# A graph layer and routed experts on one core: six counted pieces, weighed six rows a step

## The reference

```python
mems2 = layernorm(x).at[y].set(r)
keep_w = (dst != y)                                    # edges into y are dropped
nbr = top_k(-sum((mems2 - r)**2), 7)                   # seven edges nearest -> y are added
deg = segment_sum(w, col) + 2.0
dinv = rsqrt(deg)
out = segment_sum(dinv[row] * w * dinv[col] * (mems2 @ W)[row], col) + 2 * dinv**2 * (mems2 @ W)
x = x + out
idx, prb = argmax and max of softmax(layernorm(x) @ gate_w + gate_b)
pos = rank of the token within its expert              # kept if below 1954 (capacity 1.25)
x = x + (relu(h @ w1[idx] + b1[idx]) @ w2[idx] + b2[idx]) * prb * kept
```

## Time and profile before

| | us |
|---|---|
| median of 3 runs | 2663.68 (2661.24 to 2668.46) |
| profiled execution | 2664.55 |
| its span, first to last instruction | 2662.9 |
| first gather of the node phase starts | 244.0 |
| last gather of the node phase starts | 1858.9 |
| POOL busy in the span | 1582.6 (59%) |
| PE busy in the span | 1940.1 (73%) |

### The profile page before, as it was taken

One profiled execution on the slowest core, in us unless ns is written; L12 is line 12 of the kernel. 1 busy time (PEld: TensorE's weight loads), 2 busy tenths in 40 slices (PEclk: granted clock), 3 DMA queues, 4 the chain that ended last, 5 costly groups with the idle time before them and its releaser, 6 DMA issues. The chain is left out here.

```text
span 2662.9 us, 37670 instructions
## 1 busy us (share of the span) xinstructions
PE 1940.1 (73%) x11184; PEld 1685.1 (63%) x11185; DVE 1355.6 (51%) x3909; ACT 616.2 (23%) x1239; POOL 1582.6 (59%) x1644
## 2 busy tenths in 40 slices
PE   2003667776677667767767789898599899899985
PEld 1003556765566556656656678887588688788775
DVE  7969886245622651452251257776444344345443
ACT  1467000210021002102102133333223332332222
POOL 6622677777777777777777777777123422422233
PEclk8556888998899889979989999999699899899988
DMA  9135233753366346536636677876412212211211
GB/s 276 46 89 166 85 102 114 212 179 103 102 194 208 102 123 202 178 101 192 211 108 208 196 225 205 217 206 168 146 33 71 80 37 69 73 39 67 66 42 26
DMA packets 240395, 350.66 MB, mean 132 GB/s; under 512 B 47464, under 2 KB 173576, under 8 KB 240068
## 3 DMA queue, kind: packets, MB, share of 16 engines
q0 software_dynamic: 75712, 198.29, 26.0%
q1 hardware_dynamic: 163172, 148.02, 19.0%
q10 hardware_dynamic: 1312, 2.10, 0.3%
HBM read 296.73 MB, written 56.40 MB: 133 GB/s over the span
## 5 line engine op out<-in xcount | busy, mean ns | idle before, releaser
L681 POOL DMA_INDIRECT arena<-z_table,arena x1248 | 1220.1, 978 | 482.6 <-issue 374.1
L1773 PE MATMUL bank<-arena 128*128 128x128 f32 x4992 | 734.6, 309 | 336.3 <-DMA arena<-z_table,arena 171.0
L1773 PEld LDWEIGHTS bank<-arena 128*128 128x128 f32 x4992 | 682.7, 219 | 432.7 <-issue 350.8
L1239 DVE TENSOR_TENSOR nodes<-nodes,bank 128x256 f32 x312 | 131.2, 421 | 781.9 <-PE bank L1773 768.8
L741 POOL DMA_INDIRECT out<-arena x128 | 130.1, 1017 | 437.5 <-DVE arena L1654 420.8
L2021 PE MATMUL bank<-arena 128*128 128x256 f32 (+1 forms) x1472 | 332.4, 386 | 29.3 <-issue 18.2
L2021 PEld LDWEIGHTS bank<-arena 128*128 128x128 f32 x1472 | 284.9, 197 | 70.4 <-issue 31.8
L2033 PE MATMUL bank<-arena,nodes 128*128 128x256 f32 (+1 forms) x1472 | 326.0, 380 | 0.0
L818 ACT ACTIVATE arena<-arena 128x512 f32<-128x512 uint16 (+1 forms) x125 | 135.4, 1086 | 810.7 <-DVE arena L1258 463.9
L2033 PEld LDWEIGHTS bank<-arena,nodes 128*128 128x128 f32 (+1 forms) x1472 | 273.2, 188 | 39.5 <-issue 1.0
L921 ACT ACTIVATE nodes<-bank,arena 128x256 f32<-128x256 f32 (+1 forms) x368 | 152.4, 465 | 467.1 <-PE bank L2021 467.1
(11 more groups left out here) (316 smaller groups left out, 1801.2 us busy)
## 6 DMA issues: line engine op xcount, KB each, us to landing
arena<-z_table SPq DMA_DIRECT2D x120, 512.0 KB
arena<-z_table,arena POOLq DMA_INDIRECT x1248
arena<-in_L_ffn_w SPq DMA_DIRECT2D x14, 1024.0 KB, 7.6
z_table<-nodes SPq DMA_DIRECT2D x14, 896.0 KB, 6.7
x_rows<-nodes SPq DMA_DIRECT2D x98, 128.0 KB
arena<-in_x SPq DMA_DIRECT2D x48, 256.0 KB, 3.7
out<-nodes SPq DMA_DIRECT2D x96, 128.0 KB
nodes<-in_x SPq DMA_DIRECT2D x12, 896.0 KB, 11.5
```

What stands on the lines that cost most here:

```text
L681: nc.gpsimd.indirect_dma_start(gath[:, slot, t, :], None, z_table, bass.IndirectOffsetOnAxis(ap=src_idx[:, tile_at:tile_at + 1], axis=0)). ...
L1239: nc.vector.tensor_tensor(where, where, agg_bank[step % AB][:, 0:D].rearrange("p (k c) -> p k c", k=KD), ALU.add).then_inc(S["agg_added"], 1)
L1773: last = nc.tensor.matmul(agg_bank[i][:, k * P:(k + 1) * P], gath[:, i, t, k * P:(k + 1) * P], sel[:, i, t, :], start=(t == 0), stop=(t == ...
```

## The change

`PIECES` becomes 144, 64, 48, 40, 32 and 24 tiles: 352 counted tiles in place of 320, and six pieces in place of five. `HB` becomes 6: six rows per chunk, 17 chunks (the last has two rows), 16 chunk steps per piece. Piece 0 is weighed, copied out and turned as the others are; node `y` takes the place of the 128th column, and the piece's strips are clipped one node lower. `count_f`, `near_row` and `piece_rows` leave the arena and lie over a new tensor `columns`, together with sixteen node vectors of the preparation and the routing that had tensors of their own. ACT waits for `res_ok` ahead of the experts.

```diff
-    PIECES = [144, 64, 48, 40, 24]
+    PIECES = [144, 64, 48, 40, 32, 24]
-    HB = 4
+    HB = 6
...
+        columns = sb("columns", [P, 16 * NW])
+        count_f = columns[:, 0:2 * HB * P].rearrange("p (j h n) -> p j h n", j=2, h=HB)
+        near_row = columns[0:1, 0:8 * P]
+        piece_rows = columns[:, 0:KD * P].rearrange("p (k c) -> p k c", k=KD)
+        (first_f, n_less, last_hist, deg, neg_mean, rstd, shift, var2, gap2, kept, pos_lo, pos_hi, expert,
+         pos_f, part_f, row_f_i) = [columns[:, i * NW:(i + 1) * NW] for i in range(16)]
...
@@ chunk_counts (ACT)
+                nodes_in = P - 1 if p == 0 else P
                 if p == 0:
                     act.wait_ge(S["chosen_ok"], 1)
-                    nc.scalar.activation(count_f[:, j, 0:m, P], chosen[:, c * HB:c * HB + m], ACT.Copy)
-                nc.scalar.activation(count_f[:, j, 0:m, 0:P], counts[:, :, c * HB:c * HB + m].rearrange("p n h -> p h n"),
+                    nc.scalar.activation(count_f[:, j, 0:m, P - 1], chosen[:, c * HB:c * HB + m], ACT.Copy)
+                nc.scalar.activation(count_f[:, j, 0:m, 0:nodes_in],
+                                     counts[:, 0:nodes_in, c * HB:c * HB + m].rearrange("p n h -> p h n"),
                                      ACT.Copy).then_inc(S["count_ok"], 1)
@@ pieces of a step (ACT)
-                    if p:
-                        take_piece(p)
+                    take_piece(p)
@@ ahead of the experts (ACT)
+            act.wait_ge(S["res_ok"], 2)
             act.sem_inc(S["hid_ok"], FT)
@@ unit limits (DVE)
-                then(nc.vector.tensor_scalar(unit_rel[0:1, mine], unit_rel[0:1, mine], float(P - PANEL), 0.0, ALU.min, ALU.max))
+                then(nc.vector.tensor_scalar(unit_rel[0:1, mine], unit_rel[0:1, mine], float(P - PANEL - (p == 0)), 0.0, ALU.min, ALU.max))
@@ add_piece (DVE)
-                if p == 0:
-                    dve.wait_ge(S["piece_ps"], 1)
-                    total = piece_bank[:, 0:KD * (P + 1)].rearrange("p (k c) -> p k c", k=KD)
-                else:
-                    dve.wait_ge(S["piece_turned"], p)
-                    total = piece_bank[:, D:2 * D].rearrange("p (k c) -> p k c", k=KD)
+                dve.wait_ge(S["piece_turned"], p + 1)
+                total = piece_bank[:, D:2 * D].rearrange("p (k c) -> p k c", k=KD)
...
@@ weigh_chunk (PE)
                 for i in range(m):
-                    if p:
-                        last = nc.tensor.matmul(piece_bank[:, 0:D], count_f[:, j, i, 0:P], z_ring[:, j, i, :], start=False, stop=False)
-                        continue
-                    for k in range(KD):
-                        last = nc.tensor.matmul(piece_bank[:, k * (P + 1):k * (P + 1) + width], z_ring[:, j, i, k * P:(k + 1) * P],
-                                                count_f[:, j, i, 0:width], start=False, stop=False)
+                    last = nc.tensor.matmul(piece_bank[:, 0:D], count_f[:, j, i, :], z_ring[:, j, i, :], start=False, stop=False)
...
@@ end of a piece (PE)
-                if p:
-                    turn_piece(p)
+                turn_piece(p)
```

More of the change, by code:

```diff
@@ L235, in build @@
         r_rows = sb("r_rows", [P, D])
+        columns = sb("columns", [P, 16 * NW])
[4 more added lines that the diff above has]
+         pos_f, part_f, row_f_i) = [columns[:, i * NW:(i + 1) * NW] for i in range(16)]
+        pos_i, part_i, row_i = pos_f.bitcast(I32), part_f.bitcast(I32), row_f_i.bitcast(I32)
+        assert 2 * HB * P <= 16 * NW
         y_i = sb("y_i", [P, 1], I32)
@@ L299, in build @@
         z_ring = carve([2, HB, D])
[L300 to L305, removed]
         at[0] = counts_at
@@ L409, in build @@
         EDGE_TURNS = [(i, b, min(4, EB - b)) for i in range(2) for b in range(0, EB, 4)]
-        neg_mean = sb("neg_mean", [P, NW])
-        rstd = sb("rstd", [P, NW])
-        shift = sb("shift", [P, NW])
         dist = sb("dist", [P, NW])
-        deg = sb("deg", [P, NW])
-        last_hist = sb("last_hist", [P, NW])
-        first_f = sb("first_f", [P, NW])
         first_i = sb("first_i", [P, NW], I32)
-        n_less = sb("n_less", [P, NW])
         row_start = sb("row_start", [P, NW + 1])
@@ L442, in build @@
         mean2 = neg_mean
-        var2 = sb("var2", [P, NW])
-        gap2 = sb("gap2", [P, NW])
         rstd2 = rstd
@@ L448, in build @@
         norm = n_less
-        expert = sb("expert", [P, NW])
         node_half = expert
         place = last_hist
-        kept = sb("kept", [P, NW])
-        row_i = sb("row_i", [P, NW], I32)
         row_f = sb("row_f", [P, NW])
[L455 to L458, removed]
         iota_r = sb("iota_r", [P, P])
@@ L1267, in add_piece @@
                 dve.wait_ge(S["agg_added"], adds_through(step))
-                if p == 0:
-                    dve.wait_ge(S["piece_ps"], 1)
-                    total = piece_bank[:, 0:KD * (P + 1)].rearrange("p (k c) -> p k c", k=KD)
-                else:
-                    dve.wait_ge(S["piece_turned"], p)
-                    total = piece_bank[:, D:2 * D].rearrange("p (k c) -> p k c", k=KD)
-                where = agg[:, :, bass.ds(base, P)]
-                nc.vector.tensor_tensor(where, where, total[:, :, 0:P], ALU.add).then_inc(S["agg_added"], 1)
+                dve.wait_ge(S["piece_turned"], p + 1)
+                total = piece_bank[:, D:2 * D].rearrange("p (k c) -> p k c", k=KD)
+                nodes_in = P - 1 if p == 0 else P
+                where = agg[:, :, bass.ds(base, nodes_in)]
+                nc.vector.tensor_tensor(where, where, total[:, :, 0:nodes_in], ALU.add).then_inc(S["agg_added"], 1)
                 if p == 0:
@@ L1278, in add_piece @@
                     own = agg[:, :, bass.ds(ycol, 1)]
-                    then(nc.vector.tensor_tensor(own, own, total[:, :, P:P + 1], ALU.add))
+                    then(nc.vector.tensor_tensor(own, own, total[:, :, P - 1:P], ALU.add))
             def x1_pair(b, j):
@@ L1790, in weigh_chunk @@
                 j = n % 2
-                width = P + 1 if p == 0 else P
                 pe.wait_ge(S["count_ok"], q * BODY + (n + 1))
@@ L1794, in weigh_chunk @@
                 for i in range(m):
-                    if p:
-                        last = nc.tensor.matmul(piece_bank[:, 0:D], count_f[:, j, i, 0:P], z_ring[:, j, i, :], start=False, stop=False)
-                        continue
-                    for k in range(KD):
-                        last = nc.tensor.matmul(piece_bank[:, k * (P + 1):k * (P + 1) + width], z_ring[:, j, i, k * P:(k + 1) * P],
-                                                count_f[:, j, i, 0:width], start=False, stop=False)
+                    last = nc.tensor.matmul(piece_bank[:, 0:D], count_f[:, j, i, :], z_ring[:, j, i, :], start=False, stop=False)
                 last.then_inc(S["chunk_ps"], 1)
             def turn_piece(p):
-                pe.wait_ge(S["piece_out"], p)
+                pe.wait_ge(S["piece_out"], p + 1)
                 for k in range(KD):
@@ L1810, in _ @@
             for p in range(NP):
-                span = KD * (P + 1) if p == 0 else D
-                whole = piece_bank[:, 0:span]
+                whole = piece_bank[:, 0:D]
                 s0, c0, n0 = strip_step[p], chunk_step[p], UNIT0[p]
@@ L1836, in _ @@
                     pe.wait_ge(S["chosen_ok"], 1)
-                nc.tensor.matmul(whole, zeros[:, 0:P], zeros[:, 0:span], start=True, stop=False)
+                nc.tensor.matmul(whole, zeros[:, 0:P], zeros[:, 0:D], start=True, stop=False)
                 with pe.Fori(0, (PCH - 1) // BODY - 1) as q:
@@ L1846, in _ @@
                 weigh_chunk(p, p * PCH + PCH - 1, 0, NW - (PCH - 1) * HB)
-                nc.tensor.matmul(whole, zeros[:, 0:P], zeros[:, 0:span], start=False, stop=True).then_inc(S["piece_ps"], 1)
-                if p:
-                    turn_piece(p)
+                nc.tensor.matmul(whole, zeros[:, 0:P], zeros[:, 0:D], start=False, stop=True).then_inc(S["piece_ps"], 1)
+                turn_piece(p)
             R_STEPS, R_PAIRS = 2 * BODY, 2 * PAIRS_IN[0]
```

## The result

| | us | ratio to before, 95% |
|---|---|---|
| before | 2663.68 (2660.41 to 2668.86) | |
| after | 2648.06 (2635.64 to 2649.03) | 0.993 [0.9911, 0.9949] |
| after, measured again | 2643.11 (2640.53 to 2647.13) | 0.9918 [0.9905, 0.9931] |
| forecast | 2628, range 2619 to 2649 | |

The change makes the kernel faster, by 15 to 20 us where 36 were forecast. The time lies inside the stated range, at its far end, and outside the likeliest case's own range. The profiled execution of after took 2649.03 us, with a span of 2647.5, against a forecast of 2628.9 in the same terms: 20.1 us to find.

The account below looks back on a forecast made before the run. POOL's gathers were taken to pace the node phase. From the profiled 2664.55 us, -37.0 for the steps and +1.4 for the start gave 2628.9; less 0.9, 2628 us, range 2619 to 2649.

Parts of the forecast that it names:

- the likeliest case: Whole kernel: everything goes as forecast, with its own range of 2622 to 2637 us; chance 80%.
- The node phase is paced by POOL: Node phase, 244 to 1860 us: POOL sets the pace with four gathers per step over 312 steps.
- -37.0 us: Node phase: chunk steps save 120.5 us and the new strip stage adds 83.5; bounds -40 to -31.
- new strip stage: Strip stage of 16 steps added by the extra piece: 5.22 us each, +83.5 us, bounds +80 to +90.
- Chunk steps: 24 x 5.02: Chunk stages: 24 chunk steps fewer at 5.02 us each, -120.5 us.
- What lies beside the gathers, and whether it still fits: PE, z load, ACT and DVE beside POOL's gathers in the node phase: all still fit, costed at 0.
- The z load: Chunk steps: 768 in place of 512 KB still lands 1.3 us early; cost 0.
- the rival of the transfers: Chunk stages: load beside gathers makes a step take 5.25 us, +22 us, 2650 in all; chance 10%.
- The rule that I weighed: DVE's added clear: port lock could hold POOL up to 5.3 us; put at 0, upper bound 1.25 us.
- Start: Before the gathers: one more loop turn and longer vectors add 1.4 us; first gather later than 246 would show it wrong.
- They move as a block: After the gathers: 68 routing steps and the experts are the same work, with no change in their time.
- PE's clock: Chunk stages: PE drops to 1.2 GHz in denser steps, +137 us, 2765 in all; chance 6%.

Follow-up runs that it names:

- after_psum: The changed kernel with the selection's row of numbers read from PSUM (float32) in place of SBUF (bf16): 2609.65 us, ratio 0.9799.
- before_psum: The kernel before with the selection's row of numbers read from PSUM (float32) in place of SBUF (bf16): 2642.15 us, ratio 0.9918.

## Why the prediction was right and where it was wrong

- **"The node phase is paced by POOL" and "-37.0 us": right.** With the hold gone from both kernels the chunk steps take 600.3 and 480.3 us (-120.0, forecast -120.5) and the new strip stage 80.5 (forecast 83.5): -39.5. 1216 gathers, PE's 12 records in 2.75 us, ACT's copy of 1.56 us, and no wait that counts of the weighing for its load: as forecast.
- **"Chunk steps: 24 x 5.02": the term that was mis-sized.** Their number was right; their price is 5.14 after the change (5.11 when measured again), so the 96 that remain cost 11.2 us more. I took POOL's price of a step as constant because nothing that POOL waits for came late. But a gather's own duration isn't constant; it depends on what DVE runs when it starts.
- **The step that failed** is "What lies beside the gathers, and whether it still fits". I asked of PE, of the load and of DVE only whether each ends in time for what uses it. They do: POOL idles 5.8 us for PE between 449 and 1480. I put at nothing, without asking, what they do to each other. The z load ("Cost 0") is still moving when the group's rows are due, which land at 2.50 us in place of 1.79; product, add and selection follow, and the selection is 1 us later, which is most of a gather's cycle of 1.25. There it lies over gathers' starts: 11.8 us held in the chunk steps in place of 2.1.
- **That the range held is partly luck.** Its upper end, 2649, came from the rival of the transfers, whose step of 5.25 us did not come about; the time of 2648.06 is made up of held gathers and of 7 us behind them, which stood in no term. Measured again it was 2643.11.
- **The rule that I weighed was applied to the wrong instruction.** On the trace I excluded the clear, rightly: 20 gathers within clears, none longer. The Trainium skill (SBUF — State Buffer, "SBUF: two separate sides") names beside the two-port modes the case of VectorE reading two SBUF inputs against a GpSimd instruction that reads SBUF, and has it that whichever starts first keeps the ports and the other is blocked. The trace agrees where the selection starts first: 1.38 us in place of 0.95, and 0.95 with one operand in PSUM. It does not show the other order: with the gather first, the selection keeps its 0.68 us. The selection stands in every step; I named the strips' one-hots alone and counted their price as paid. They are 11 us, the selection 31.2. The earlier trace rows had the hint: 0.98 us per gather in the strips and 0.95 in the chunk stages, which I noted and priced by stage without asking for its cause.
- **"The transfers set the chunk step", 2650 us: its time was met, its mechanism only in part.** The larger load does make the gathers' rows land later, but that costs nothing by itself: with the same loads and the same late landing (2.53 us) the step is 5.00 in after_psum.
- **The new strip stage** cost 81.2 us where I had 83.5: inside its bounds, 2 us on the good side.
- **Start:** the first gather came at 246.8 us, beyond the 246 that I had named as a sign of being wrong. The loop's turn is the 1.2 to 1.3 us forecast (68.65 to 69.9 in after); the other 1.4 us arose around it.
- **"They move as a block": off by 7 us in this execution**, about 4 in the mean over all profiles; open.
- PE's clock stayed at 0.96 to 1.00 in all chunk stages: that rival was rightly small.

## What to carry to other kernels

Where POOL's DMA issues pace a phase, read their own duration (mean ns per group) as well as their waits: a mean that differs between stages is a cost with a cause. Then look at what DVE runs when a gather starts, and give DVE instructions that read two SBUF operands one of them in PSUM; here this brought more (33 to 38 us) than the change of the schedule (16 to 20). An edit that "fits" beside the bounding engine can still shift the phase of an instruction that disturbs it, so ask not only whether it ends in time, but what it does to the arrival of its neighbours' data.

## What the runs showed of the hardware

- A VectorE `tensor_tensor` with both inputs in SBUF (0.69 us) and an indirect DMA's issue on POOL don't run side by side when VectorE was first: the issue is lengthened from 0.95 to 1.47 us (once 1.61), and behind four such instructions in a row (0.41 us each) to 2.23. When POOL was first, neither is longer: the selections of after take 0.68 to 0.76 us wherever they fall. The border lies between 0.034 and 0.036 us after the selection's recorded start.
- The same instruction with one operand in PSUM takes the same 0.68 us and holds nothing. A clear of 5.29 us holds nothing either. A one-hot of 0.35 us with one tensor input (f16, to bf16) does hold: 0.12 us on average in some 90 cases.
- 768 KB loaded in each step beside the gathers (235 GB/s in a chunk stage of after_psum) did not lengthen a step at all: 5.00 us, as with 512 KB in before_psum. They did delay the landing of the gathered rows, from 1.79 to 2.53 us behind the fourth gather's end (median of the chunk steps, before and after_psum).
